# A two-pass convolution and whitening kernel: the intermediate y stored in 4 KB runs by two transfers of 64 partitions, output in whole tiles, and all stores issued by ScalarE

## What is computed

```python
# x: (4 images, 64 channels, 256, 256) f32
hx, hy = implicit_filter(...)              # one row filter and one column filter per channel
k = einsum('ijk,imk->ijmk', hx, hy)        # so the 2-D filter is separable
y = irfft2(rfft2(x, 512x512) * k_f)[..., :256, :256]   # causal 2-D convolution
x = y + x * bias[:, None, None]
# layer 1: whitening over the 64 channels
x1 = transpose(x, (1, 0, 2, 3)).reshape(64, -1)
x1_s = x1[:, ::9]                          # every ninth pixel
cov = x1_s @ x1_s.T / n + 0.01 * I
deconv = newton_schulz_isqrt(cov, 5)
out = deconv @ (x1 - mean(x1_s))           # back to (4, 64, 256, 256)
```

## Time and profile before

| | us |
|---|---|
| median of 3 runs | 992.02 (989.27 to 993.87) |
| the profiled execution | 994.94 |
| its span | 993.1 |
| PE / DVE / POOL / ACT busy in the span | 881.0 / 574.7 / 496.4 / 397.8 |
| first pass, up to the last Toeplitz matmul | 0 to 662 |
| last covariance and matrix iteration | 662 to 702 |
| second pass | 702 to 993 |

### The profile page before, as it was taken

One profiled execution on the slowest core, in us unless ns is written; L12 is line 12 of the kernel. 1 busy time (PEld: TensorE's weight loads), 2 busy tenths in 40 slices (PEclk: granted clock), 3 DMA queues, 4 the chain that ended last, 5 costly groups with the idle time before them and its releaser, 6 DMA issues.

```text
span 993.1 us, 15420 instructions
## 1 busy us (share of the span) xinstructions
PE 881.0 (89%) x5904; PEld 731.0 (74%) x5904; DVE 574.7 (58%) x642; ACT 397.8 (40%) x714; POOL 496.4 (50%) x277
## 2 busy tenths in 40 slices
PE   1799999999999999999999999977997777777896
PEld 0799999999999999999989899976432222222342
DVE  4487788778787657677767676771222222222332
ACT  2455555555555435454444444420121222222332
POOL 2488888889898747777767677760000000000000
PEclk9999999999999999999999999997799999999999
DMA  3799999999999959999999999975499999999999
GB/s 100 161 286 272 275 309 270 268 296 287 282 292 272 298 154 312 320 304 315 309 312 300 296 298 317 312 264 214 142 425 425 427 426 425 426 427 426 362 326 287
DMA packets 147301, 303.39 MB, mean 306 GB/s; under 512 B 10619, under 2 KB 109084, under 8 KB 132636
## 3 DMA queue, kind: packets, MB, share of 16 engines
q1 hardware_dynamic: 147228, 302.41, 92.1%
HBM read 167.96 MB, written 134.41 MB: 304 GB/s over the span
## 4 chain that ended last, share of the span: by engine, by line
PE 47%; DMA 41%; DVE 8%; SPq 2%; issue 1%; ACT 1%; POOL 0%; DVEq 0%; ACTq 0%
DMA convolved<-y_all 24%; DMA out<-z_all 14%; PE ps L601 12%; PE ps L687 10%; PE ps L598 7%; PE ps L599 7%; PE ps L600 7%; DVE y_all L477 4%; PE ps L630 3%; DMA out<-masked_all 2%; DVE z_all L578 1%; SPq L204 1%; ACT z_all L409 1%; DMA plain<-filters 0%; SPq L265 0%
## 5 line engine op out<-in xcount | busy, mean ns | idle before, releaser
L598 PE MATMUL ps<-rounded 128*128 128x256 f32 x1024 | 373.9, 365 | 24.6 <-issue 15.3
L337 POOL TENSOR_TENSOR masked_all<-y_all,mask 128x1024 f32<-128x1024 f32 x127 | 328.8, 2589 | 80.0 <-DVE y_all L477 79.7
L599 PE MATMUL ps<-rounded 128*128 128x256 f32 x1024 | 288.3, 282 | 0.0
L600 PE MATMUL ps<-rounded 128*128 128x256 f32 x1024 | 288.3, 282 | 0.0
L477 DVE SCALAR_TENSOR_TENSOR y_all<-x_all,bias_sb,ps 128x1024 f32<-128x1024 f32 x127 | 162.5, 1280 | 139.9 <-DMA convolved<-y_all 131.7
L598 PEld LDWEIGHTS ps<-rounded 128*128 128x128 f32 x1024 | 197.3, 193 | 30.7 <-issue 30.1
L308 POOL TENSOR_TENSOR rounded<-x_all,rounded 128x512 fp32r<-128x512 f32 x128 | 165.2, 1290 | 88.6 <-ACT rounded L370 87.4
L601 PE MATMUL ps<-plain,x_all 128*128 128x128 f32 x1024 | 197.9, 275 | 0.0
L599 PEld LDWEIGHTS ps<-rounded 128*128 128x128 f32 x1024 | 197.5, 193 | 0.0
L601 PE MATMUL ps<-plain 128*128 128x128 f32 x1024 | 196.7, 274 | 0.0
L600 PEld LDWEIGHTS ps<-rounded 128*128 128x128 f32 x1024 | 193.3, 189 | 0.0
(11 more groups left out here) (98 smaller groups left out, 471.4 us busy)
## 6 DMA issues: line engine op xcount, KB each, us to landing
x_all<-x SPq DMA_DIRECT2D x128, 512.0 KB, 6.9
convolved<-y_all SPq DMA_DIRECT2D x128, 512.0 KB, 8.0
out<-z_all SPq DMA_DIRECT2D x96, 512.0 KB, 12.7
plain<-filters SPq DMA_DIRECT2D x128, 256.0 KB, 9.1
kept<-convolved SPq DMA_DIRECT2D x29, 1024.0 KB, 18.9
out<-masked_all SPq DMA_DIRECT2D x32, 512.0 KB, 12.8
kept<-convolved SPq DMA_DIRECT2D x56, 256.0 KB, 9.5
rounded<-convolved SPq DMA_DIRECT2D x9, 1024.0 KB, 18.8
```

The lines of the kernel that those rows point to most:

```text
L337: nc.gpsimd.tensor_tensor(masked_of(k, 0, PER), by_image(y_sb[k]), mask_of(q // C, 0, PER), ALU.mult).then_inc(masked_done, 1)
L598: mm(wide, hi[:, b, cols], t_hi[k][:, f, :], start=True, stop=False)
L599: mm(wide, hi[:, b, cols], t_lo[k][:, f, :], start=False, stop=False)
L600: mm(wide, lo[:, b, cols], t_hi[k][:, f, :], start=False, stop=False)
```

## The change

1. `y_dram` is laid out as 128 rows (half h of the 128 image rows, channel) per sweep. Each such row holds 64 image rows x 1024 floats, 256 KB. `store_y` sends each half of `y_sb`'s partitions (64 x 4 KB) to one contiguous piece of 256 KB: two transfers, with 128 packets of 4 KB together, where there were 512 of 1 KB.
2. A tile of the second pass is now two image rows of each half for both images of a sweep; its 128 partitions of 8 KB lie 256 KB apart. `load_kept` moves halves of a tile (512 KB, rows of 4 KB) at every second unit, not quarters at every unit.
3. The output is a tensor of 64 whole tiles, stored by one transfer of 128 partitions each, contiguous in HBM. The host puts the order right afterwards.
4. ACT issues both kinds of stores on its own queue: `store_y(q-1)` after `flip(q+2)`, where it waits for `y_done`; in the second pass the store of tile t comes after ACT's own half, and ACT waits for its own and DVE's half before it goes on to tile t+1. SP only loads.

```diff
-            def store_y(q):
-                k = q % 2
-                wait(sp, y_done, q + 1)
-                dst = bass.AP(tensor=y_dram.tensor, offset=(q // C) * BLOCKS * C * P * S + (q % C) * P * S,
-                              ap=[[S, P], [C * P * S, BLOCKS], [1, S]])
-                sp.dma_start(dst, y_sb[k].rearrange("p (i w) -> p i w", w=S)).then_inc(y_stored[k], 16)
...
             def tile_in(t, lo, hi):
-                image, rows = t // (P // TROWS), t % (P // TROWS)
-                return bass.AP(tensor=y_dram.tensor, offset=image * HB * C * P * S + rows * TW + lo,
-                               ap=[[P * S, HB * C], [1, hi - lo]])
+                sweep, rows = t // SWEEP_TILES, t % SWEEP_TILES
+                return bass.AP(tensor=y_dram.tensor, offset=sweep * P * ROWS * XW + rows * TW + lo,
+                               ap=[[ROWS * XW, P], [1, hi - lo]])
...
             for q in range(UNITS):
                 load_x(q + 4)
-                store_y(q - 1)
                 load_hankel(q + 5)
                 load_kept(q)
...
-            for t in range(TILES):
-                if t + slots < TILES:
-                    sp.wait_ge(t_mm[1], t + 1)
-                    load_tile(t + slots)
-
-                sp.wait_ge(t_act, t + 1)
-                sp.wait_ge(t_dve, t + 1)
-                store_tile(t)
+            for t in range(TILES - slots):
+                sp.wait_ge(t_mm[1], t + 1)
+                load_tile(t + slots)
...
+            def store_y(q):
+                if q < 0:
+                    return
+                k = q % 2
+                act.wait_ge(y_done, q + 1)
+                for h in range(2):
+                    dst = bass.AP(tensor=y_dram.tensor, offset=((q // C) * P + h * C + q % C) * ROWS * XW,
+                                  ap=[[XW, ROWS], [1, XW]])
+                    act.dma_start(dst, y_sb[k][h * ROWS:(h + 1) * ROWS, :]).then_inc(y_stored[k], 16)
+
             for q in range(UNITS):
                 round_v(q)
                 round_x(q + 2)
                 flip(q + 2)
+                store_y(q - 1)
+            store_y(LAST)
...
+                act.wait_ge(t_act, t + 1)
+                act.wait_ge(t_dve, t + 1)
+                act.dma_start(out[t], t_out[t % O_SLOTS]).then_inc(t_stored[t % O_SLOTS], 16)
```

More of the change, by code:

```diff
@@ L45 @@
 X_SLOTS, T_SLOTS, H_SLOTS = 5, 3, 3
-TROWS = 8
-TW = TROWS * S
-TILES = B * (P // TROWS)
+ROWS = P // 2
+TROWS = 2
+TW = TROWS * XW
+SWEEP_TILES = ROWS // TROWS
+TILES = SWEEPS * SWEEP_TILES
 KEPT = 14
-PIECES = 4
+PIECES = 2
 O_SLOTS = 4
@@ L57, in conv_whiten @@
     g_dram = nc.dram_tensor("filters", [2 * C, GLEN], F32, kind="Internal").ap()
-    y_dram = nc.dram_tensor("convolved", [B * HB * C, P * S], F32, kind="Internal").ap()
+    y_dram = nc.dram_tensor("convolved", [SWEEPS * P, ROWS * XW], F32, kind="Internal").ap()
     with ExitStack() as ctx:
@@ L214, in load_hankel @@
                 sp.dma_start(hankel[k], src).then_inc(hankel_loaded[k], 16)
[L216 to L223 removed]
             def tile_in(t, lo, hi):
[L226 to L228 removed]
+                sweep, rows = t // SWEEP_TILES, t % SWEEP_TILES
+                return bass.AP(tensor=y_dram.tensor, offset=sweep * P * ROWS * XW + rows * TW + lo,
+                               ap=[[ROWS * XW, P], [1, hi - lo]])
             def load_kept(q):
[L231 to L232 removed]
+                n = (q - (C + 4)) // 2
+                if q % 2 or not 0 <= n < KEPT * PIECES:
                     return
@@ L237, in load_kept @@
                 for k in range(2):
-                    sp.wait_ge(y_stored[k], 16 * (C // 2))
+                    sp.wait_ge(y_stored[k], 32 * (C // 2))
                 sp.dma_start(kept[:, n * w:(n + 1) * w], tile_in(n // PIECES, lo, lo + w)).then_inc(kept_loaded, 16)
@@ L258, in load_tile @@
                 sp.dma_start(t_in[t % slots], tile_in(t, 0, TW)).then_inc(t_loaded[t % slots], 16)
[L260 to L265, removed]
             sp.wait_ge(y_mm, UNITS)
@@ L270, in _ @@
                 load_tile(t)
-            store_y(LAST)
+            sp.wait_ge(y_done, UNITS)
             for t in range(after_v, after_y):
@@ L274, in _ @@
             for k in range(2):
-                sp.wait_ge(y_stored[k], 16 * (UNITS // 2))
+                sp.wait_ge(y_stored[k], 32 * (UNITS // 2))
             sp.wait_ge(masked_done, LAST)
@@ L279, in _ @@
                 load_tile(t)
-            for t in range(TILES):
-                if t + slots < TILES:
-                    sp.wait_ge(t_mm[1], t + 1)
-                    load_tile(t + slots)
-                sp.wait_ge(t_act, t + 1)
-                sp.wait_ge(t_dve, t + 1)
-                store_tile(t)
+            for t in range(TILES - slots):
+                sp.wait_ge(t_mm[1], t + 1)
+                load_tile(t + slots)
             for k in range(O_SLOTS):
-                sp.wait_ge(t_stored[k], 16 * HB * (TILES // O_SLOTS))
+                sp.wait_ge(t_stored[k], 16 * (TILES // O_SLOTS))
         @block.gpsimd
@@ L405, in _ @@
                 act.wait_ge(t_mm[0], t + 1)
-                wait(act, t_stored[t % O_SLOTS], 16 * HB * (t // O_SLOTS))
+                wait(act, t_stored[t % O_SLOTS], 16 * (t // O_SLOTS))
                 src = ps[:, bank(t, 0):bank(t, 0) + 2, :].rearrange("p r n -> p (r n)")
@@ L472, in finish_y @@
                 k = q % 2
-                wait(dve, y_stored[k], 16 * (q // 2))
+                wait(dve, y_stored[k], 32 * (q // 2))
                 wait(dve, masked_done, q - 1)
@@ L514, in finish_half @@
                                                mask_of(SWEEPS - 1, b, 1), ALU.mult)
-            dve.wait_ge(y_stored[last_y], 16 * (LAST // 2))
+            dve.wait_ge(y_stored[last_y], 32 * (LAST // 2))
             dve.wait_ge(masked_done, LAST - 1)
@@ L574, in _ @@
                 dve.wait_ge(t_mm[1], t + 1)
-                wait(dve, t_stored[t % O_SLOTS], 16 * HB * (t // O_SLOTS))
+                wait(dve, t_stored[t % O_SLOTS], 16 * (t // O_SLOTS))
                 src = ps[:, bank(t, 1):bank(t, 1) + 2, :].rearrange("p r n -> p (r n)")
@@ L714 @@
            for k, v in arrays.items()]
-    out = nc.dram_tensor("out", [B, C, S, S], F32, kind="ExternalOutput").ap()
+    out = nc.dram_tensor("out", [TILES, P, TW], F32, kind="ExternalOutput").ap()
     conv_whiten(nc, *aps, out)
     r = run_bass_kernel_spmd(nc, [arrays], core_ids=[0])
-    return r.results[0]["out"]
+    tiles = r.results[0]["out"].reshape(SWEEPS, SWEEP_TILES, 2, C, TROWS, PER, HB, S)
+    return np.ascontiguousarray(tiles.transpose(0, 5, 3, 6, 2, 1, 4, 7)).reshape(B, C, S, S)
```

## The result

The change makes the kernel a little slower. Over 20 runs of each, the median goes from 991.9 to 998.6 us; the ratio is 1.006, with a 95% interval of 1.004 to 1.008. Forecast was 967.

A forecast was written before the change was run, and what follows sets the result against it. It took PE to bound the first sweep, the two-buffer y ring the second, and the DMA ceiling, then PE, the second pass. Gains of 23.2 + 1.5 = 24.7 us from the median 992.0 gave 967, range 957 to 986.

The forecast's parts named there:

- The ring of two buffers: Second sweep before: finish_y, issue and landing of y stores ask 10.2 us per two units, where PE asks 9.3.
- the line: DMA packet cost, a straight line: 0.024 us per packet plus 0.0347 per 1,000 B; 0.060 for 1 KB, 0.166 for 4 KB.
- part (1): y in 4 KB runs, with tile halves: second sweep reaches PE's first-sweep pace, 23.2 us less; first sweep gains nothing.
- Part (2): y store on another queue: landing of 5 to 6 us, two-buffer ring takes 7.2 to 8.1 of 9.28; no term.
- Part (3): ACT's new y-store issues: 0.86 us per unit, 3.68 of 4.64 in all, nothing on PE's path: 0.
- rival A: ACT sets the first pass's pace once an issue costs over 0.91 us; at 1.192, 1036 us; 11%.
- Part (5): Second pass: same bytes at the DMA ceiling, only the very end changes: 1.5 us less, between 0 and 3.
- B: Half stores of y are slower per byte: 973 to 986 us, 12%; at twice the time both sweeps lose, about 1045, 2%.
- C: Second pass: output stores on their own queue get ahead of loads, up to 20 us more gain, 947 to 955; 9%.
- D: Second pass: tile loads with rows 256 KB apart are a little slower, 970 to 980 us; 4%.
- E: Second sweep: x's landing grows by what y's shrinks, pace stays near 5.04 us per unit, 986 to 992; 3%.

The follow-up runs named there:

- before_3y: The kernel before with three y buffers and 13 kept tiles, nothing else changed: 981.7 us, 1.4% faster than the kernel before.
- queue_alone: The kernel before with its one y transfer of 1 KB rows issued by ACT, at the changed kernel's place: 0.5% slower than the kernel before.
- whole_act: The changed kernel with each y unit stored in one transfer of 128 partitions x 4 KB, still on ACT, rows reordered: 970.8 us, 0.977 of the kernel before.
- y_on_sp: The changed kernel with the two half stores of y issued by SP behind the x load, the rest as changed: 1.000 of the kernel before.

## Why the prediction was wrong

*What bounds the kernel.* The ring of two buffers in the second sweep was read rightly, and before_3y shows it. The first sweep was rightly called bound by PE, but its ring was then left out. It had 9.2 us of 9.28. The row that would have said so is the wait of `finish_y` for stores in the first sweep (before, 100 to 330 us), which I had not put beside rows 2:

```profile
DVE y_all L477 <- DMA convolved<-y_all: 43.3, 38, 2.7
```

*What a packet costs.* The share of 98% was taken for work. before_3y did 4.88 us per unit where the line gave 4.96 as the least. And in the trace of before, from 370 to 640 us, the 4 KB packets of the x loads took 0.206 us on average but 0.159 in the middle, so the share seems to have waiting in it. What y's packets take can be read directly where the store has a queue of its own, in queue_alone with 1 KB packets and in whole_act with 4 KB packets. The DMA view of 100 to 330 us (queue, packets, MB moved, share of the 16 engines), first for queue_alone:

```profile
q10 hardware_dynamic: 25864, 25.69, 31.6%
```

The same for the change:

```profile
q10 hardware_dynamic: 7480, 24.52, 26.3%
```

And for whole_act:

```profile
q10 hardware_dynamic: 7169, 26.11, 27.8%
```

A unit of y is 0.524 MB, so these are 49.0, 46.8 and 49.8 units. A unit's store takes 0.316 x 230 x 16 / 49.0 = 23.7 us of one engine in 1 KB packets, 20.7 as two halves and 20.5 whole, semaphore writes included. That is 0.046 us per 1 KB packet where the line had 0.060, and 0.160 per 4 KB packet where it had 0.166. So 4 KB runs save 3.2 us of one engine per unit, 0.2 us over 16, and part (1) had 9.3, or 0.58 over 16. The two halves cost the engines no more than the whole: what halves cost in the kernel shows in the landing and not in this share.

*Part (1), 23.2 us.* Measured are 9.7 us less in the second sweep of the change and 15.5 in that of whole_act. The term was too large, since it took the sweep to PE's pace and counted 1 KB packets too dear. That whole_act's total comes out within 4 us of the forecast is luck: 6.6 us too few up to the second pass and 5.9 too many in it nearly cancel. And packets aren't needed for most of such a gain: before_3y, with the 1 KB packets left as they were and a third buffer, has 13.4 us less in its second sweep.

*Part (2), the step that failed.* It took 5 to 6 us for the landing and two issues of 0.43, 7.2 to 8.1 of 9.28 with `finish_y`, and called the ring closed in time. Measured are 8.2 us from `y_done` to the last landing, 9.5 with `finish_y`, and the first sweep, which was given no term, lost 17.4 us. That loss is larger than all that the second sweep gained. Three sizes were wrong in it. An issue of a half took 0.556 us on ACT, not 0.43. A half of 64 neighbours takes 0.7 us longer than one of every second partition when stores are alone; in the kernel the last landing is 8.2 for 7.7, and what makes that difference there isn't shown. And sharing the engines with x and the Hankel block, packet by packet, isn't shorter than waiting behind x and ahead of the Hankel block: even the whole transfer lands after 7.0 us, not 5 to 6. The bounds were there, 2.9 and 8.0; the value was taken at the wrong end.

*Part (3), ACT's work: 0.* The issues take 1.1 us of ACT per unit, 3.9 of 4.64 in all, under the point of rival A. But the sum took `y_done` as punctual. When `finish_y` waits up to 2.3 us for a store, ACT waits with it and `round_v` is late. y_on_sp, against the change, puts ACT's place at 0.7%, queue_alone at 0.5%.

*Part (5), the second pass.* 6.5 us for 1.5. The last store lands 4.4 us after its issue (988.9 to 993.3), where it was 6.6 before (986.5 to 993.1): 2.2 of it. In the first 22 us of the stage 258 GB/s are moved for 229, 0.64 MB more, which is some 1.5 us at 427 GB/s; there tile loads no longer wait in SP's program behind the stores, and a whole store is issued in 0.34 us, not twice 0.83. Which of these two counts, and where the remaining 2.8 us lie, wasn't measured.

*The rivals.* B named halves, and halves of neighbours are slower when stores are alone. But in the kernel their packets took the engines no longer (20.7 us per unit for 20.5 whole), so B's price by packets didn't come; the halves' landing did the harm, and in the first sweep, which B's likelier case spared. A's point wasn't reached (0.556 for 0.91). C and D didn't come: 427 GB/s up to 930, and from 960 to 970 PE's pace of before at 303 GB/s. E didn't: x lands after 6.0 us for 6.9. The slower end needed no single rival to be strong: small delays met a ring with little to spare, and ACT's queue passed them on.

## What to carry to other kernels

A stage that one engine fills may have a ring behind it that is just as full. Before moving or splitting a store, add up its ring (wait, issue, landing of the last part, the instruction that refills) for every stage, and compare it with the pace. Cheaper packets need not shorten a landing by as much: what frees a buffer is the last landing. Here one transfer over all 128 partitions beat two of 64 neighbours, and one more buffer brought back nearly as much as the whole transfer did (0.979 for 0.977), in the first sweep. A total that comes out right can hide terms that don't, so compare stage by stage. And a wait that is moved to a busy engine's queue brings along all the lateness of what it waits for.

## What the runs showed of the hardware

With no loads under way, a store of 256 KB from 64 neighbouring partitions, one of a pair, landed after 3.1 us, one of 512 KB from 128 after 2.6, one of 256 KB from every second partition, also one of a pair, after 2.4. Beside loads in the kernel a 4 KB packet of a y store took 0.16 us whether the store came as two halves or whole, and a 1 KB packet 0.046. Issuing a half took ACT 0.54 to 0.56 us, issuing a whole transfer of 128 partitions in rows of 4 or 8 KB 0.33 to 0.36. The DMA share of 16 engines read 1.00 at 157 groups in 100 us, and 1.02 at 164 groups with the same packets: it tells that packets are under way, not that no more would go.
